# Sixth sum of weight blocks built from four loaded pieces, in place of one piece and a sum read back from DRAM

## What is computed

```python
def _sage_layer(h, edge_src, edge_dst, deg_inv, W_self, W_neigh, b):
    msg = h[edge_src]
    agg = jax.ops.segment_sum(msg, edge_dst, num_segments=h.shape[0])
    mean = agg * deg_inv[:, None]
    return h @ W_self + mean @ W_neigh + b
...
    h = jax.nn.relu(_sage_layer(x, edge_src, edge_dst, deg_inv, W_self0, W_neigh0, b0))
    out = _sage_layer(h, edge_src, edge_dst, deg_inv, W_self1, W_neigh1, b1)
    return out
```

## Time and profile before

| | before |
|---|---|
| time, median of 3 runs | 1013.62 us (1012.4 to 1013.89) |
| profiled execution | 1011.6 us |
| its span, first to last instruction | 1009.7 us |
| TensorE matmuls busy | 946.7 us (94%) |
| VectorE busy | 741.9 us (73%) |
| ScalarE busy | 451.1 us (45%) |
| GpSimd busy | 225.4 us (22%) |
| mean granted TensorE clock | 0.98 |
| last stage | from 394.0 us |

### The profile page before, as it was taken

One profiled execution on the slowest core, in us unless ns is written; L12 is line 12 of the kernel. 1 busy time (PEld: TensorE's weight loads), 2 busy tenths in 40 slices (PEclk: granted clock), 3 DMA queues, 4 the chain that ended last, 5 costly groups with the idle time before them and its releaser, 6 DMA issues.

```text
span 1009.7 us, 14407 instructions
## 1 busy us (share of the span) xinstructions
PE 946.7 (94%) x4630; PEld 766.5 (76%) x4630; DVE 741.9 (73%) x1732; ACT 451.1 (45%) x864; POOL 225.4 (22%) x344
## 2 busy tenths in 40 slices
PE   5899998989898998999998999999899999999996
PEld 3477788878788886777776777788777777777774
DVE  7999955383747987689944889933689866889854
ACT  4788743161526477543422343444443422343323
POOL 3000103841454332132321122011132101122000
PEclk9699999999999999999999999999999999999998
DMA  6258783895013484554989353365254287355585
GB/s 214 62 99 217 190 201 81 201 204 108 0 43 127 147 296 171 163 178 146 191 257 281 98 168 128 98 215 178 82 168 144 87 302 244 104 167 175 157 264 159
DMA packets 60733, 164.52 MB, mean 163 GB/s; under 512 B 20223, under 2 KB 21232, under 8 KB 60456
## 3 DMA queue, kind: packets, MB, share of 16 engines
q0 software_dynamic: 19968, 76.09, 26.9%
q1 hardware_dynamic: 33498, 71.64, 24.5%
q10 hardware_dynamic: 7182, 15.66, 4.6%
HBM read 137.29 MB, written 51.82 MB: 187 GB/s over the span
## 4 chain that ended last, share of the span: by engine, by line
PE 62%; DVE 11%; ACT 6%; issue 5%; DMA 4%; POOL 1%; ACTq 0%; SPq 0%; DVEq 0%; POOLq 0%
PE bank L2138 32%; PE bank L2154 16%; PE bank L1155 5%; PE bank L1123 5%; ACT squares L1350 2%; DMA w_piece<-w_neigh 2%; DMA at_dram<-a_turned 1%; PE bank L669 1%; DVE h_stage L1900 1%; DVE dec_z L1434 1%; PE bank L633 1%; DMA w_piece<-w_self 1%; PE bank L2167 1%; DVE w_slot L2004 1%; ACT res L1830 1%
## 5 line engine op out<-in xcount | busy, mean ns | idle before, releaser
L2138 PE MATMUL bank<-w_slot,h_stage 128*125 128x512 f32 x1680 | 395.7, 397 | 6.8 <-DVE h_stage L1900 6.8
L2138 PEld LDWEIGHTS bank<-w_slot,h_stage 128*125 128x125 f32 x1680 | 313.0, 187 | 87.6 <-DVE h_stage L1900 9.1
L2154 PE MATMUL bank<-g_rows,a_stage 125*125 125x512 f32 x800 | 189.3, 396 | 0.9 <-issue 0.5
L2154 PEld LDWEIGHTS bank<-g_rows,a_stage 125*125 125x125 f32 x800 | 147.0, 185 | 39.6 <-issue 3.5
L1800 ACT ACTIVATE w_slot<-w_piece 128x512 fp32r<-128x512 f32 x104 | 65.1, 632 | 175.0 <-DVE w_piece L1993 83.5
L1695 POOL DMA_DIRECT2D w_piece<-w_neigh x96 | 51.8, 541 | 197.0 <-DVE w_slot L2004 85.8
L2055 DVE SCALAR_TENSOR_TENSOR o<-bank,deg_inv,o 125x512 f32<-125x512 f32 x40 | 30.0, 751 | 79.5 <-PE bank L2154 79.5
L1695 POOL DMA_DIRECT2D w_piece<-w_self x72 | 39.4, 548 | 197.7 <-DVE w_slot L2004 182.9
L2004 DVE TENSOR_TENSOR w_slot<-w_piece,w_slot 128x512 fp32r<-128x512 f32 x104 | 70.4, 684 | 7.7 <-ACT w_slot L1800 7.7
L1155 PE MATMUL bank<-a_turned,gn 125*128 125x418 f32 x360 | 70.8, 354 | 3.9 <-DVE gn L1015 2.4
L1155 PEld LDWEIGHTS bank<-a_turned,gn 125*128 125x128 f32 x360 | 66.9, 188 | 5.7 <-DVE gn L1015 3.5
(11 more groups left out here) (238 smaller groups left out, 1335.0 us busy)
## 6 DMA issues: line engine op xcount, KB each, us to landing
a_stage<-at_dram SPq DMA_DIRECT2D x40, 625.0 KB, 5.4
w_piece<-w_neigh POOLq DMA_DIRECT2D x96, 256.0 KB, 3.7
w_piece<-w_self POOLq DMA_DIRECT2D x72, 256.0 KB, 3.0
at_dram<-a_turned SPq DMA_DIRECT2D x10, 625.0 KB, 11.8
dec_y<-x_bd SPq DMA_DIRECT2D x10, 512.0 KB, 4.1
dec_x<-x_ob SPq DMA_DIRECT2D x10, 512.0 KB, 4.6
x_dram<-h_rows SPq DMA_DIRECT2D x10, 512.0 KB, 3.0
x_dram<-sage_b POOLq DMA_DIRECT2D x10, 512.0 KB, 11.9
```

The lines of the kernel that those rows point to most:

```text
L2138: mm = pe.matmul(bank(q, i)[0:NT, :], st[m % 3][:, a, k, :], slots[w % 3][:, b, k, :], start=(k == 0 and p == 0), stop=(k == HK - 1 and p ...
L2154: mm = pe.matmul(ps_a[u][0:NT, :], cast(a_st[t % 3][0:NT, k, :]), cast(g[0:NT, h, k, :]), start=(n == 0 and h == 0), stop=(n == T - 1 and ...
```

## The change

Set 5 is made from four pieces, b21, b22, b12 and b11, with three sums: b21 - b22, b12 - b11, and the sum of the two. `PIECES`, the pieces per block, goes from 2 to 4 for set 5; `SUMS` counts the sums per block for the semaphore. The write of set 3's result to DRAM, its DRAM tensor, the read and the waits for it go.

```diff
--- before.py
+++ after.py
@@ -1500,7 +1500,8 @@
     JOBS = [(prod, r) for prod in PRODUCTS for r in range(HT)]
     NJ, SETS = len(JOBS), len(PRODUCTS)
     PLACE = {job: i for i, job in enumerate(JOBS)}
-    PIECES = (1, 1, 1, 3, 2, 2, 2)
+    PIECES = (1, 1, 1, 3, 2, 4, 2)
+    SUMS = (0, 0, 0, 2, 1, 3, 1)
     FIRST_SET = 2
     RING = 5
     ROWS = ((0, 120), (120, NT))
@@ -1517,7 +1518,6 @@
     o_out = [sem("o_out0"), sem("o_out1")]
     piece_in = [sem(f"piece_in{n}") for n in range(RING)]
     (w_sum, SUM0), (w_hi, HI0), (w_lo, LO0) = s.spent[0:3]
-    t_out = [s.spent[3], s.spent[18]]
     (f_step, STEP0), (f_var, VAR0), (f_root, ROOT0), (f_norm, NORM0), (f_normed, NORMED0) = s.spent[4:9]
     x2_in, both_in = s.spent[9:14], s.spent[15:18]
     x2_biased = sem("x2_biased")
@@ -1584,7 +1584,7 @@
     def sum_order(w, k):
 
         q, i = divmod(w, SETS)
-        return 20 * q + {3: 2 * k, 4: 8 + k, 5: 12 + k, 6: 16 + k}[i]
+        return HK * (sum(SUMS) * q + sum(SUMS[0:i])) + SUMS[i] * k
 
     def pieces_until(w, k):
 
@@ -1694,10 +1694,6 @@
         def load(n, source):
             pool.dma_start(piece[n % RING][:, :], source).then_inc(piece_in[n % RING], 16)
 
-        def wait_spill(q, k):
-            landed, base = t_out[k % 2]
-            pool.wait_ge(landed, base + 16 * (2 * q + k // 2 + 1))
-
         def freed(n):
 
             if n < 0:
@@ -1707,12 +1703,9 @@
                     j = n - pieces_until(w, k)
                     if not 0 <= j < PIECES[w % SETS]:
                         continue
-                    if w % SETS == 3 and j == 2:
-                        wait_spill(w // SETS, k)
-                    if w % SETS == 3 and j == 0:
-                        pool.wait_ge(w_sum, SUM0 + sum_order(w, k) + 2)
-                    elif j == 1:
-                        pool.wait_ge(w_sum, SUM0 + sum_order(w, k) + 1)
+                    order = {(3, 0): 2, (3, 1): 1, (4, 1): 1, (5, 1): 1, (5, 2): 3, (5, 3): 2, (6, 1): 1}.get((w % SETS, j))
+                    if order:
+                        pool.wait_ge(w_sum, SUM0 + sum_order(w, k) + order)
                     else:
                         pool.wait_ge(w_lo, LO0 + halves_order(w, k) + 1)
 
@@ -1721,13 +1714,9 @@
             q, i = divmod(w, SETS)
             layer, hf = QUARTERS[q]
             w_self, w_neigh = io["w_self"][layer, hf], io["w_neigh"][layer, hf]
-            if i == 5:
-                wait_spill(q, 2)
-                wait_spill(q, 3)
             for k in range(HK):
                 b11, b12, b21, b22 = w_self[k], w_neigh[k], w_self[HK + k], w_neigh[HK + k]
-                t2 = io["t2_dram"][q, k]
-                sources = ((b11,), (b21,), (b22,), (b12, b11, b22), (b22, b12), (b21, t2), (b12, b11))[i]
+                sources = ((b11,), (b21,), (b22,), (b12, b11, b22), (b22, b12), (b21, b22, b12, b11), (b12, b11))[i]
                 for j, source in enumerate(sources):
                     n = pieces_until(w, k) + j
                     if n == 3:
@@ -1793,13 +1782,11 @@
             else:
                 act.wait_ge(p_done, NJ * before + HT * last + HT)
             if i in (3, 4, 5, 6):
-                act.wait_ge(w_sum, SUM0 + sum_order(w, k) + (2 if i == 3 else 1))
+                act.wait_ge(w_sum, SUM0 + sum_order(w, k) + SUMS[i])
                 source = halves_piece(w, k)
             else:
                 source = piece_of(act, w, k, 0)
             act.activation(slots[w % 3][:, 0, k, :], source[:, :], ACT.Copy).then_inc(w_hi, 1)
-            if i == 3:
-                act.dma_start(io["t2_dram"][q, k], source[:, :]).then_inc(t_out[k % 2][0], 16)
 
         def at_job(q, i):
 
@@ -1991,6 +1978,11 @@
             first = piece_of(dve, w, k, 0)
             second = piece_of(dve, w, k, 1)
             dve.tensor_tensor(first[:, :], first[:, :], second[:, :], ALU.subtract).then_inc(w_sum, 1)
+            if i == 5:
+                third, fourth = [piece_of(dve, w, k, j) for j in (2, 3)]
+                dve.tensor_tensor(third[:, :], third[:, :], fourth[:, :], ALU.subtract).then_inc(w_sum, 1)
+                dve.wait_ge(w_sum, SUM0 + sum_order(w, k) + 2)
+                dve.tensor_tensor(first[:, :], first[:, :], third[:, :], ALU.add).then_inc(w_sum, 1)
             if i == 3:
                 third = piece_of(dve, w, k, 2)
                 dve.wait_ge(w_sum, SUM0 + sum_order(w, k) + 1)
@@ -2325,7 +2317,7 @@
           for name, a in arrays.items()}
     for name, shape in (("at_dram", (T, 128, T, NT)), ("x2_dram", (T, 128, D)), ("h1_dram", (T, 128, D)),
                         ("x_bd", (N + 128 - NT, D)), ("x_ob", (N + 128 - NT, D)),
-                        ("t2_dram", (4, 4, 128, 512)), ("y_dram", (T, 128, 512))):
+                        ("y_dram", (T, 128, 512))):
         io[name] = nc.dram_tensor(name, shape, F32, kind="Internal").ap()
     io["out"] = nc.dram_tensor("out", (N, D), F32, kind="ExternalOutput").ap()
     program(nc, io)
```

## The result

| | before | after |
|---|---|---|
| median of the runs | 1013.01 us (1011.39 to 1013.89, 4 runs) | 1091.09 us (1089.72 to 1092.11, 4 runs) |
| span of the profiled execution | 1009.7 us | 1089.8 us |
| mean granted clock | 0.980 | 0.949 |

The ratio is 1.0772, with a 95% interval from 1.0752 to 1.0792: slower by 78 us, where 66 were forecast (1079, range 1055 to 1102). On another chip the pair gave 1.0760 (1.0735 to 1.0785).

What follows compares the result with a forecast made beforehand. TensorE was taken as the bound, with VectorE having only 7 to 11% to spare. To the median of 1013.6 us came 59.3 for the ring and 6.4 for the clock, some 66: 1079 us, range 1055 to 1102.

Steps and rivals of the forecast that it cites:

- The mechanism: Sixth set's loads, five-place ring: later pieces wait until the previous block's weight low frees a place, stalling VectorE, then TensorE.
- the main case: Ring waits in the sixth set plus a short clock dip: 1079 us, own range 1068 to 1090, chance 0.70.
- rival (b): Clock stays low after each gap, jobs 24 and 25 at half speed, 5.2 us a quarter: 1094 us, chance 0.17.
- What it removes is worth 0: Dropping the spill's writes and GpSimd's waits for them gains between 0 and 0.4 us, taken as 0.
- Rival (a): Pieces arrive in time, only VectorE's added sums cost: 15 to 18 us in all, 1030 us, chance 0.10.
- The start of the chain: End of the sixth set's first weight low: 5.4 us after job 18 starts in the third quarter, 8.2 in the first.
- the extra lateness: First quarter: VectorE runs later, so all that follows shifts by 2.8 us, making 16.8 instead of 14.0.
- The round trip: Sixth set, from one block's weight low to the next's: 7.8, 8.6 and 8.0 us against TensorE's 2.79 a job.
- the landing: Time from a piece's load issue to its arrival: 3.1 us (2.9 to 3.2), the term with the widest ends.
- the ring's 59.3 us: TensorE's waits from the sixth set's ring over four quarters: 16.8, 14.0, 14.0 and 14.5 us.
- The clock's term: TensorE's granted clock dipping after the long gaps: 1.6 us a quarter, 6.4 in all.
- The estimate from the Trainium skill: Landing of a 256 KB load by the page's fit, some 2.6 us: 6 us less in all, 1073 us.

Runs made afterwards that it cites:

- e3_result_last: Changed kernel with the sixth set's result in its last loaded piece instead of its first, same loads and sums: 1038.67 us, ratio 1.0292 to the kernel before.
- e4_own_places: Changed kernel with four buffers of their own for the sixth set's third and fourth pieces, so the ring carries two a block: 1026.99 us, ratio 1.0173.
- e2_no_spill: Kernel before without the spill's write, read and waits, the plain block b22 read instead: 1009.04 us against 1009.26, ratio 0.999.
- e1_sums_only: Kernel before with two more VectorE sums per block of the sixth set, loads, spill and ring kept: 1025.85 us against 1009.26, ratio 1.0178.
- runs with filled gaps: Changed kernel with unused matmuls in TensorE's gaps before jobs 22 to 24: 1082.50 us (52 a quarter), 1080.59 us (44), ratios 1.0711 and 1.0706.

## Why the prediction held, and which terms were short

The mechanism held, and the sum was 12 us short (66 forecast, 78 measured). The measured 1091 lies in the stated range, but just outside the 1068 to 1090 that the main case had for itself, and nearer to rival (b)'s 1094 than to 1079. The number alone would have spoken for (b); the traces speak against it.

- The mechanism, that three of four pieces of a block wait for the weight low of the block before, was right: shown by `e3_result_last` and `e4_own_places`, which keep loads and sums and change only who has to free a place.
- "What it removes is worth 0": shown (`e2_no_spill`).
- Rival (a), only the sums count, was given 15 to 18 us for that part. The part costs 17 to 18 (`e1_sums_only`), and it isn't the whole.
- The start of the chain held: weight_low(0) of the third quarter ends at 807.42, 5.3 us after the start of job 18 (802.16); 5.4 were forecast. In the first quarter it ends at 463.32, 7.9 us after (455.40), where 8.2 were forecast, so the extra lateness there was real. That the last quarter would cost 0.5 more for a slow piece did not show: the forecast's 14.0, 2.6 for its longer trips and 2.5 for the clock make 19.1, and it cost 18.8.
- The round trip was mis-sized. Forecast were 7.8, 8.6 and 8.0 us, 24.4 a quarter. The trips of the third quarter are 9.05, 9.73 and 8.79, 27.6; over the four quarters they sum to 109.1 against 97.6. The term that was short is the landing: 3.1 us was read from loads issued in pairs, and there are four in a row now, of which the third is the one waited for. It landed in 4.4 us in the burst shown (3.5 to 4.4 over the quarters). I had seen that the fourth, the next block's first piece, "takes a place freed long before", and had not counted it as traffic in the same burst. The pitch of the dependent sum was 0.72, not 0.79. With the trips as measured the ring's 59.3 us become 70.8. The wider end of the forecast had a landing of 3.9, read where the spill's writes ran beside the loads; here it came with no spill at all, so the size was allowed for, and its cause was not.
- The clock's term was short by 2.5 us of 8.9. 1.6 us a quarter was taken; the 132 matmuls from job 24 on took 33.31, 32.42, 33.35 and 33.41 us where `e1_sums_only` needs 30.90, so 2.4, 1.5, 2.5 and 2.5, 8.9 in all against 6.4. The runs with filled gaps bear out only some 6 of it, so as a price the 6.4 was about right. 70.8 and 8.9 make 79.7, beside 79.0 between the traces; that this fits so well is partly luck. Two dips that are in no term nearly cancel: 1.5 us at the start of the third quarter's products, which the trace before lacks, and the 1.6 us behind the gap of 3.10 us ahead of the second quarter's, which the trace after lacks.
- Rival (b), low in jobs 24 and 25 throughout, would have cost 5.2 a quarter: it did not come. In the third quarter the clock was back at 1.00 from 841.1 on, 5.5 us after job 24 began. The row taken for (b), 0.51 "for 7 us", is a window that starts inside the idle time: from the gap's end at 401.92 the clock was low for some 5 us there too. The clock fell at each of jobs 22, 23 and 24 of every quarter, so at job 22 too, where a gap of 2.8 was forecast and 3.5 to 5.9 came; what fell on jobs 22 and 23 was hidden by the wait behind them. The Trainium skill ("TensorE: Matmul & The Clock Gate", "HAM oscillation — how this bites in real kernels") tells of a kernel in which each wait for a load made the next tile start cold, and the trace agrees: behind each of the twelve gaps (3.5 to 5.9 us) the clock was at 0.50 from the job's start, or within half a us of it.
- The length of a gap does not foretell the dip by itself, as the prediction had taken it to ("after 2.38 us it stayed at 1.00"). After the same 2.38 us ahead of the third quarter's products the clock fell in the trace of every other run, and after the same 3.10 us ahead of the second quarter's it fell in the kernel before and not in `e1_sums_only` (61.52 us for 22 jobs). Why is not shown here.
- The estimate from the Trainium skill ("DMA: Bandwidth & Descriptors", "Anatomy of one DMA — SWDGE (gpsimd) path"), 1073, was further off than the rows: the page's fit is per load, 2.6 us for 256 KB, and here four follow each other and land in 2.9 to 4.5 us.

## What to carry to other kernels

When a change makes a block need more pieces than the ring can prefetch, ask of every piece which instruction frees its place and how far ahead of its use that is; here the added loads were cheap, and the order in which places came free was not. Put a result into the buffer that is loaded last, so that the operands' places are refilled as each sum ends: that alone gave back some 48 of 78 us here. And a landing time holds only for the number of loads that stood in a row when it was read.

## What the runs showed that was not expected

Four loads of 256 KB from GpSimd's queue in a row, 0.53 us apart, landed 2.9, 3.1, 4.4 and 4.5 us after their issue, so the third came almost 2 us after the second although it was issued 0.5 us later; with three in a row the third took 3.5 in the burst shown, and 3.2 to 4.0 over the sixteen of two runs. The first two read the one weight matrix and the last two the other, but that is hardly it: in `e3_result_last` loads of the latter (`w_self`) landed in 2.9 and 3.4 us. Why the step lies between the second and the third was not found.
